# Working up to four gathered groups of the next tile ahead of the x3 turn in a one-core graph layer kernel

## The reference

```python
xn = _layernorm(x)
# graph part
h_self, h_neigh = xn @ W_self, xn @ W_neigh
h_sparse = _maxk(h_neigh, 32)                       # keep the 32 largest of each row
summed = segment_sum(h_sparse[src], dst)            # the gather
neigh = summed / maximum(deg, 1.0)[:, None]
# linear attention with a gate
k = softmax(k, axis=nodes); context = k^T v; out = q @ context
gate = sigmoid(gelu(ln(xn) @ Wg1 + bg1) @ Wg2 + bg2)
x = x + h_self + neigh + (out * gate @ Wproj + bproj)
# feed-forward on the half of the nodes with the largest router weight
xn2 = _layernorm(x); w = xn2 @ wr + br
y = (gelu(xn2 @ w1 + b1) @ w2 + b2) * w             # for the chosen nodes, otherwise 0
return x + y + xn2
```

## Time and profile before

| | before |
|---|---|
| median of 3 runs | 1930.84 us (1927.08 to 1932.76) |
| the profiled execution | 1927.08 us, span 1925.3 us |
| PE busy | 1498.3 us (78%) |
| DVE busy | 1215.4 us (63%) |
| POOL busy | 1208.1 us (63%) |
| ACT busy | 438.9 us (23%) |
| mean granted TensorE clock | 0.881 |

### The profile page before, as it was taken

The page is one execution under the profiler, slowest core; times in us unless marked ns, Lnnn a source line. Parts: engine busy times, 40 slices in busy tenths (PEclk is TensorE's granted clock), DMA queues, the critical chain, the costliest instruction groups (busy, mean ns, idle before and its releaser), DMA issues. The chain is left out here.

```text
span 1925.3 us, 38962 instructions
## 1 busy us (share of the span) xinstructions
PE 1498.3 (78%) x8607; PEld 1105.2 (57%) x8608; DVE 1215.4 (63%) x3823; ACT 438.9 (23%) x974; POOL 1208.1 (63%) x1349
## 2 busy tenths in 40 slices
PE   1698643986677867797887789987899988999871
PEld 0354333554445555666565567765677766777661
DVE  4899991885555633286664358863468843787457
ACT  0354322011111111121222122221223322333220
POOL 2154554377777777767777757777757775677400
PEclk9799866997778878798998789987999998999995
DMA  9122114133333357524346734447624475344755
GB/s 213 31 82 77 59 54 131 39 106 109 109 108 111 110 145 188 141 86 120 109 118 171 186 86 116 117 120 195 174 84 123 125 198 151 99 118 133 182 132 153
DMA packets 150922, 236.26 MB, mean 123 GB/s; under 512 B 26369, under 2 KB 115421, under 8 KB 150781
## 3 DMA queue, kind: packets, MB, share of 16 engines
q0 software_dynamic: 52480, 142.82, 26.9%
q10 hardware_dynamic: 70374, 65.55, 13.4%
q1 hardware_dynamic: 27926, 26.20, 5.6%
HBM read 208.46 MB, written 26.01 MB: 122 GB/s over the span
## 5 line engine op out<-in xcount | busy, mean ns | idle before, releaser
L656 POOL DMA_INDIRECT ring<-rows_d,stage x1088 | 1084.9, 997 | 420.2 <-issue 306.4
L1009 PE MATMUL bank<-ring,region_v 128*125 x1260 | 424.5, 450 | 172.9 <-SPq L555 147.6
L1009 PEld LDWEIGHTS bank<-ring,region_v 128*125 x1260 | 187.4, 149 | 319.0 <-issue 245.0
L1465 DVE TENSOR_SCALAR col_deg<-bank 125x1 f32<-125x1 f32 x50 | 7.9, 158 | 447.9 <-PE bank L1089 437.6
L1373 DVE SCALAR_TENSOR_TENSOR region_v<-iota,tile_start,dstT 128x500 f16 x315 | 230.3, 740 | 35.4 <-issue 12.8
L970 PE MATMUL bank<-region_v 128*125 128x256 f32 x848 | 230.6, 432 | 19.6 <-issue 19.6
L1400 DVE TENSOR_SCALAR region_k<-iota,win_start,region_k 128x500 f16 x622 | 226.3, 405 | 0.0
L1010 PE MATMUL bank<-ones,region_v 128*125 128x2 f16 x1260 | 218.7, 174 | 0.0
L970 PEld LDWEIGHTS bank<-region_v 128*125 128x125 f32 x848 | 179.9, 218 | 51.5 <-issue 20.3
L963 PEld LDWEIGHTS bank<-region_v 128*128 128x128 f32 x1664 | 195.5, 193 | 2.8
L963 PE MATMUL bank<-region_v 128*128 128x125 f32 x1664 | 195.7, 276 | 0.0
(11 more groups left out here) (284 smaller groups left out, 1952.0 us busy)
## 6 DMA issues: line engine op xcount, KB each, us to landing
region_k<-rows_d ACTq DMA_DIRECT2D x30, 672.0 KB
ring<-rows_d,stage POOLq DMA_INDIRECT x1088
region_k<-rows_d ACTq DMA_DIRECT2D x10, 784.0 KB
region_v<-xT_d ACTq DMA_DIRECT2D x53, 125.0 KB, 4.7
xT_d<-region_r ACTq DMA_DIRECT2D x51, 125.0 KB, 2.1
rows_d<-region_r SPq DMA_DIRECT2D x50, 125.0 KB
region_k<-in_x_dram ACTq DMA_DIRECT2D x50, 125.0 KB
yw_d<-region_v ACTq DMA_DIRECT2D x50, 125.0 KB
```

What stands on the lines that cost most here:

```text
L656: pool.indirect_dma_start(out=ring[:, c, :], out_offset=None, in_=rows_d, in_offset=bass.IndirectOffsetOnAxis(ap=stage[:, c:c + 1], axis=0 ...
L1009: m = pe.matmul(total, onehot_s, row_s, start=False, stop=False, skip_group_check=True)
```

## The change

A constant `LEAD` of 4 groups is added. A new table in `bounds` holds for each position the end of its lead, the smaller of g0 + 4 and g1. PE visits the groups g0 up to that end before `turn_x3` and the windows, and divides only what is left among the parts. DVE writes the one-hots of these groups one position earlier, in `hot_ahead`: after its register loads and before its wait for `s_agg`; for position 0 it writes them ahead of the loop. Position s = 9 has no visits, so nothing is led into it. Both engines load one more register value per position. The line numbers after the change are 4 higher on PE and up to 28 higher on DVE.

```diff
--- before.py
+++ after.py
@@ -74,6 +74,7 @@
     GC = 4
     RING = 8
     HOT = 8
+    LEAD = HOT // 2
     AHEAD = RING // 2 * GC
     ROUNDS = -(-E // (CHUNK * GC * RING))
     BLOCKS = ((0, 20), (20, 20), (40, 10))
@@ -116,8 +117,8 @@
 
     T_G0, T_G1, T_FIRST, T_VIS, T_WIN = 0, NT, 2 * NT, 3 * NT, 4 * NT
     T_PASSES = T_WIN + ND * NW + 1
-    T_ROUNDS, T_START, T_DENSE, T_GENERAL = (T_PASSES + n for n in range(1, 5))
-    T_END = T_GENERAL + 1
+    T_ROUNDS, T_START, T_DENSE, T_GENERAL, T_LEAD = (T_PASSES + n for n in range(1, 6))
+    T_END = T_LEAD + NT + 1
     NEDGE = ND * NW + 1
 
     with ExitStack() as ctx:
@@ -241,6 +242,7 @@
         row_b = region_r.take([1, NT + 1])
         row_w = region_r.take([1, NEDGE])
         win_first = region_r.take([1, NEDGE])
+        lead = region_r.take([1, NT])
         edge_row = region_r.take([1, ND + 1, NW])
         sorted_t = region_r.take([1, 4 * NT])
         general_t = region_r.take([1, 4 * NT])
@@ -415,19 +417,21 @@
 
 
             def __init__(self, engine):
-                self.engine, self.end, self.ahead, self.visits = engine, None, None, None
+                self.engine, self.end, self.ahead, self.visits, self.lead = engine, None, None, None, None
 
             def enter(self, n, s):
 
                 if s == 0:
                     self.end, self.visits = load(self.engine, n), load(self.engine, n + T_VIS)
                     self.ahead = load(self.engine, n + T_G1)
+                    self.lead = load(self.engine, n + T_LEAD)
                 g0, self.end = self.end, self.ahead
-                return g0, self.end, self.visits + (s + 1)
+                return g0, self.end, self.visits + (s + 1), self.lead
 
             def look_ahead(self, n, last):
                 if not last:
                     self.ahead = load(self.engine, n + 1 + T_G1)
+                    self.lead = load(self.engine, n + 1 + T_LEAD)
 
         def count_bank(k):
             return bank[(1, 6)[k % 2]][0:T, 0:KEYS]
@@ -1022,16 +1026,19 @@
             general = load(pe, T_GENERAL, 0, 1)
             spans = Windows(pe)
             def position(n, i, s, windows):
-                g0, g1, finals = ends.enter(n, s)
+                g0, g1, finals, led = ends.enter(n, s)
                 total = agg_bank(s)
                 here, one, two = pe.snap(n), pe.snap(n + 1), pe.snap(n + 2)
 
                 def gathered(turn):
                     parts = window_parts(windows)
                     sums = SUMMED[s][1:] if turn and s in SUMMED else ()
+                    with pe.If(led > g0):
+                        with pe.Fori(g0, led) as g:
+                            visit(finals, g, True, total)
                     if turn:
                         turn_x3(one)
-                    cuts = cut(pe, g0, g1, len(parts) + len(sums))
+                    cuts = cut(pe, led, g1, len(parts) + len(sums))
                     for at, (first, end) in enumerate(zip(cuts, cuts[1:])):
                         if at < len(parts):
                             count_window(i, *parts[at])
@@ -1245,7 +1252,11 @@
             dve.tensor_scalar(bounds[:, T_ROUNDS:T_ROUNDS + 1], misc[:, 3:4], -1.0, float(ROUNDS), ALU.mult, ALU.add)
             dve.tensor_copy(bounds[:, T_START:T_START + 1], misc[:, 3:4])
             dve.tensor_copy(bounds[:, T_DENSE:T_DENSE + 1], misc[:, 0:1])
-            dve.tensor_copy(bounds[:, T_GENERAL:T_GENERAL + 1], general).then_inc(s_bounds, 1)
+            dve.tensor_copy(bounds[:, T_GENERAL:T_GENERAL + 1], general)
+            dve.memset(bounds[:, T_LEAD + NT:T_LEAD + NT + 1], 0)
+            a = st.mark(dve.tensor_scalar(lead, bounds[:, T_G0:T_G0 + NT], float(LEAD), None, ALU.add))
+            st.after(a)
+            dve.tensor_tensor(bounds[:, T_LEAD:T_LEAD + NT], lead, bounds[:, T_G1:T_G1 + NT], ALU.min).then_inc(s_bounds, 1)
             dve.wait_ge(s_std, 2)
             dve.reciprocal(gate_scale[:, 0:NT], stdg).then_inc(s_gs, 1)
             dve.wait_ge(s_small, SMALL)
@@ -1421,9 +1432,24 @@
             ends = Ends(dve)
             first_group = load(dve, T_FIRST, 0, NG)
             general = load(dve, T_GENERAL, 0, 1)
+            led = load(dve, T_LEAD)
+            with dve.If(led > 0):
+                with dve.Fori(0, led) as g:
+                    visit(1, g, tile_at(0, 0) * 4)
+            def hot_ahead(n, i, s):
+
+                if s == PER - 1:
+                    first, finals = load(dve, n + (T_G0 + 1)), load(dve, n + (T_VIS + 1)) + 1
+                    led = load(dve, n + (T_LEAD + 1))
+                else:
+                    first, finals, led = ends.end, ends.visits + (s + 2), ends.lead
+                after = dve.snap(tile_after(i, s, 1) * 4)
+                with dve.If(led > first):
+                    with dve.Fori(first, led) as g:
+                        visit(finals, g, after)
 
             def position(n, i, s, windows):
-                g0, g1, finals = ends.enter(n, s)
+                g0, g1, finals, led = ends.enter(n, s)
                 if s == 0:
                     spans.look(i, windows)
                 after_windows = range(windows.stop, windows.stop + SHARE[(s + 1) % PER])
@@ -1434,7 +1460,7 @@
                 def gathered():
                     parts = window_parts(windows)
                     at4 = dve.snap(tile * 4)
-                    cuts = cut(dve, g0, g1, len(parts))
+                    cuts = cut(dve, led if s < PER - 1 else g0, g1, len(parts))
                     for at, (first, end) in enumerate(zip(cuts, cuts[1:])):
                         if at < len(parts):
                             window(i, *parts[at])
@@ -1461,6 +1487,8 @@
                 ends.look_ahead(n, s == PER - 1)
                 if s + 1 < PER:
                     spans.look(i, after_windows)
+                if s != PER - 2:
+                    hot_ahead(n, i, s)
                 dve.wait_ge(s_agg, one)
                 dve.tensor_scalar(col["deg"][:], deg_sum[:, 0:1], 1.0, None, ALU.max).then_inc(s_deg, 1)
                 c = st.mark(dve.tensor_copy(junk, total[:, 0:C]))
```

## The result

The changed kernel takes 1939.9 us (median of 19 executions, 1932.6 to 1946.0), the kernel before, timed beside it, 1926.8 us (19, 1919.6 to 1941.0). The ratio is 1.0061 with a 95% interval of 1.0044 to 1.0078: slower by 0.6%, 8 to 15 us. Forecast were 1942 us, and slower. The profiled execution of the changed kernel took 1940.0 us with a span of 1938.2, 12.9 more than the span before.

The account below looks back on a forecast made before the run. POOL's gathers were taken to bound positions 1 to 8, PE with DVE close beside it positions 30 to 35. Terms -10.9 - 0.8 + 15.6 - 5.5 + 12.0 + 0.5 = +10.9 us gave 1938, as a median 1942 us; range 1919 to 1957.

Parts of the forecast that it names:

- part 5: DVE in the PE-bound stretches of blocks 3 and 4: loads and one-hots lengthen its period, partly reaching PE, +12 us.
- Part 1: Position 0: the first visit comes sooner, so POOL starts 10.9 us earlier, all arriving at the end of position 8: -10.9 us.
- the third rival: Early slots don't help: PE uses up its slack in positions 0 and 1 and part 1 is lost; 1953 us, chance 0.12.
- Part 2: Restarts of each block, where the ring stands full again: earlier first visits less the added register load, -0.8 us.
- Part 3: Pieces at s = 7 and 8: the third piece's load comes later with the turn, uncovered by two visits; +15.6 us.
- the mark of over 5 us: Sign for part 3: the wait for the third piece in positions 37, 38, 47 and 48 is over 5 us.
- the 1.7 of the rule: Clock cost in part 3 by the skill's rule: each of the six positions pays 1.7 us on top of its 2.2.
- Part 4: Pieces issued at s = 6: later loads let position 36's late gather go first; with losses in blocks 0 to 2, -5.5 us.
- The bound of 5.0: In part 5, four visits in hand at the turn let DVE be late by about 5.0 us before PE waits.
- The first rival: DVE's delay never reaches PE because the four visits in hand hide it; 1930 us, the same, chance 0.19.
- Part 6: Three small DVE instructions ahead of `s_bounds`: +0.5 us.
- The fourth rival: The longer loop body costs instruction fetches, +10 to +20 us if on the path; about 1955 us, chance 0.08.

Follow-up runs that it names:

- the early load: The changed kernel with ACT issuing the third piece's load ahead of its copy of the turned x3: 1901.8 us, ratio 0.9898 to the kernel before.
- the one with the packed word: Changed kernel with the third piece loaded ahead of the copy, plus last group and led count in one table word: 1893.3 us, 0.9838 of the kernel before.
- `none_dve`: The kernel before plus DVE's side of the change alone, number of led groups 0: ratios 1.0016 and 0.9975 on two slower chips.

## Why the forecast was right, and where not

The total, 1942 against 1939.9, is closer than its parts, and that is luck. The loop in the profiled execution grew by 3.8 us where the parts sum to 10.9, since part 5 was nearly three times too large; 9.1 us in the search, which no part had, made up for it.

**Part 1 (-10.9): right.** -10.7 at the end of position 8. POOL's bound carried it through eight positions, so the third rival is out.

**Part 2 (-0.8): right within what can be seen.** The differences across positions 10 and 20 are -1.5 and -0.9, across 30 and 40 +0.3 and +1.3.

**Part 3 (+15.6): the mechanism right; the size agrees, in part by luck.** The six positions grew by 0.2, 4.3, 4.5, 1.8, 2.9 and 2.5 us, 16.2 in all, while their waits grew by 13.7 (from 2.5 to 3.4 us each to 4.7 to 6.0; the mark of over 5 us misses in position 48). The load no longer hides behind two visits, and it hangs on the turn by nothing but ACT's order: issued ahead of the copy, all waits but 3.7 us are gone. The size is less sure. The kernel with no group led, where turn and load stand as before, lost 9.8 us in the same six positions, and the one not led at s = 7 and 8 lost 2.6. How much of the 16.2 would have come without the displaced load stays open.

The clock was sized at 0.4 us each. All six third pieces now run at the lower level: five take 2.8 us and one 2.45 for what takes 1.47. By the Trainium skill (TensorE: Matmul & The Clock Gate, "HAM oscillation"), in whose example every wait on DMA between bursts throttles the next, the trace agrees for the waits of 4.7 to 6.0 us here; of the shorter ones in the same six positions of the kernel before, not each did so. There the third pieces took 2.82, 1.52, 1.52, 1.54, 2.09 and 2.82 us. The 16.2 us less 13.7 leave 2.5 us, 0.4 a position, by which PE is busy longer, not the 1.7 of the rule: half of the six had paid for it before.

**Part 4 (-5.5): the size right, the reason too narrow.** Position 36 gives 6.2 us. In the kernel before, the group's last gather is issued 15.0 us into the position, behind the two loads (12.4 to 13.7), and lands after 7.1 us (both counted from the end of the issue). In the changed kernel it is issued at 11.1, ahead of loads that now come at 16.7, and lands after 2.6. But with no group led it is issued at 12.8 beside loads at 12.4, lands after 3.9, and position 36 takes 18.9 us too. PE was slower there in positions 31 to 35 and POOL further ahead. So what counts is the distance of POOL to PE, and leading is one way to it. Positions 16 and 26 lost 3.1 and 2.6 us, where two groups now meet the loads; I had 1.3 for these.

**Part 5 (+12.0): the mechanism right, the size wrong: 4.5.** PE lost 2.1 us in positions 31 to 35 and 2.4 in 41 to 45. Two numbers of the step failed. DVE's own need for five positions is 113.0 us, not 115.3: an excess of 5.5 and not 7.8. And the slack was 3.2, not 1.8: DVE enters position 40 only 2.1 us behind, not 3.2, and PE feels it when the lag passes 5.3. The bound of 5.0 was near, its place was not: I had PE's last visits, but the first to wait is the mix (L933). In position 45 PE is free for it 7.1 us behind its sum, and begins it 1.8 us behind L1493. So PE waits 1.0 and 1.7 us once in each block, not "over 1 us in positions 42 to 45"; that mark of the forecast missed, while the other (no wait of DVE for the sum) holds for positions 39 to 46. Its third mark, periods that stay near 21.3, would have counted against it: they are 22.5, 21.5, 21.6 and 23.3 in positions 42 to 45, before 22.1, 21.2, 20.9 and 21.3, so it is met in two of four. With the early load, which uses the slack up, PE takes 113.6, all that DVE needs.

What the step did not see is that time is lost there with nothing led: the kernel with no group led pays 3.1 and 4.3 us in the two stretches, more than the changed one. If that is DVE's load, as the traces suggest, the four visits in hand hide part of what it costs. The first rival, DVE's delay hidden, is wrong as a rule and half right for this kernel.

**Part 6 (+0.5)** can't be told: position 0 ends 0.9 us sooner.

**Not forecast: +9.1 in the search.** Measured, the parts are -10.7, -0.7, 16.2, -6.2 and 4.5, which make +3.1; what is left of the loop (positions 16 and 26 against gains in blocks 1 and 2) is +0.7. The search in the profiled execution adds 9.1, of which 7.6 is PE busy longer at a lower mean clock. In the traces of the seven other kernels that ran at ordinary speed, the one before among them, it takes 76.5 to 80.2 us, so 86.9 is the exception. Yet the medians differ by 12 to 13 us too, and 3.8 with an ordinary search would lie under the interval of 8 to 15. The other 18 executions have no trace; whether they lose in the loop or in the search stays open. The fourth rival, code fetches, is not borne out as fetches: with no group led the new code alone costs 0.6%, some 12 us, which is about its size. But the search takes 80.0 us there with nearly the same code, PE's "issue" idle at the four back edges of the loop is 20.6 us against 16.5 before (18.3 in the changed kernel), and the six positions that lose most have no such gap of over 0.25 us. So fetches on PE can hold some 4 us of it.

## What to carry to other kernels

When a step is moved ahead of another, look for what the other one releases on a third engine: here a transfer hung on the turn through the order of ACT's program alone, and moving its issue (which in the old order brought 0.3%) turned a loss of 0.6% into a gain of 1.0%. On an engine that has no idle time, price register loads in a loop like compute (0.73 us each here), and try packing what is loaded together into one word. Build the new code with its effect switched off, and look at every stretch: here that kernel lost as much as the change, 9.8 us of it where none was expected. A delay on a nearly bound engine comes through as its excess less the slack of the first instruction that waits for it; find that instruction, and the lag at which it bites, in the trace.

## What the runs showed of the hardware

- A register load with its range check takes 0.73 us of DVE's sequencer, and loads in a row don't overlap: four take 2.9 us. The Trainium skill (Runtime: NRT & Kernel Launch, "Instruction fetch mechanics") has about 200 ns per register for a TENSOR_LOAD that reads from HBM; here it reads a table in SBUF, and the trace has 0.30 us for that instruction alone.
- A group of gathers lands 1.8 us after its last issue when nothing else moves, and 6.6 to 8.0 us after it as the first group issued behind the two loads of pieces (positions 16, 26 and 36, the eight kernels at ordinary speed). Both are counted from the end of the issue.
- On two chips the kernel before took 35 to 36% longer and the one with the packed word 33%, with "issue" gaps, mostly of 0.3 to 5 us, between PE instructions that need nothing. The same page and section says that crossing into the next block of instructions is mostly hidden; the kernel before has 31.9 us of such gaps in its trace, `none_dve` on the slower chip 657 us, and no run shows whether they are such crossings. A ratio measured there (0.961 for the kernel with the packed word) is not the one measured elsewhere (0.984).
